# A ring of four decay buffers, PSUM evictions on VectorE, and one more identity product in each attention step of the first batch

## The reference

```python
x = x + gt_a * attention(modulated_norm(x))          # 16 heads of 16, causal
x = x + gt_m * (gelu(modulated_norm(x) @ W1 + b1) @ W2 + b2)
h, gate = adaln(x)                                   # second layer
x = x + gate * (ssm(h, fwd) + flip(ssm(flip(h), bwd)))
h, gate = adaln(x)
x = x + gate * ((silu(h @ w1) * (h @ w2)) @ w3)

def ssm(h):                                          # D_INNER 512, D_STATE 64
    xs, z = split(h @ in_w); xs = silu(xs)
    dt = softplus(xs @ xproj_w[:, :512] + dt_bias); Bm, Cm = the next 64 + 64 columns
    hst = hst * exp(dt * A) + (dt * xs) * B_t        # for each token and each of 64 states
    y_t = sum over states of hst * C_t
    return ((y + xs * D) * silu(z)) @ out_w
```

## Time and profile before

| | us |
|---|---|
| median of 3 runs | 3508.55 |
| lowest, highest | 3505.45, 3510.58 |
| the profiled execution | 3518.37 |
| its span, first to last instruction | 3516.6 |
| first scan starts | 213.1 |
| first batch's attention | 24.1 to 121.3 |

### The profile page before, as it was taken

One profiled execution on the slowest core, in us unless ns is written; L12 is line 12 of the kernel. 1 busy time (PEld: TensorE's weight loads), 2 busy tenths in 40 slices (PEclk: granted clock), 3 DMA queues, 4 the chain that ended last, 5 costly groups with the idle time before them and its releaser, 6 DMA issues.

```text
span 3516.6 us, 70442 instructions
## 1 busy us (share of the span) xinstructions
PE 3076.9 (87%) x21944; PEld 2674.0 (76%) x21944; DVE 2871.4 (82%) x3123; ACT 3087.7 (88%) x6821; POOL 2942.1 (84%) x1552
## 2 busy tenths in 40 slices
PE   8788898898988899898988989899898889988776
PEld 5567787787777788787877878778777778877765
DVE  2259988899888988789987998879988899789885
ACT  1279999999889999899998998999988999999995
POOL 0059988899888998889888998889988899899995
PEclk6689999999999999999999999999999999999999
DMA  4011111111111111111111111111111111111111
GB/s 168 0 37 45 46 41 47 40 52 43 41 47 47 45 44 41 46 47 46 42 40 49 48 45 40 48 39 52 44 40 48 47 45 43 42 42 44 53 48 27
DMA packets 163039, 162.55 MB, mean 46 GB/s; under 512 B 17610, under 2 KB 156874, under 8 KB 162644
## 3 DMA queue, kind: packets, MB, share of 16 engines
q1 hardware_dynamic: 162644, 157.69, 16.2%
HBM read 154.44 MB, written 3.18 MB: 45 GB/s over the span
## 4 chain that ended last, share of the span: by engine, by line
POOL 30%; PE 27%; issue 25%; ACT 12%; DVE 6%; POOLq 1%; DVEq 0%; ACTq 0%; DMA 0%; SPq 0%
POOL hst L409 23%; POOL uBT L418 7%; PE ps L1228 6%; PE ps L1244 6%; ACT dA L584 5%; PE ps L997 4%; ACT uBT L570 3%; DVE hst L899 3%; PE ps L1006 2%; PE ps L1066 2%; PE ps L1044 1%; PE ps L1117 1%; PE ps L1053 1%; PE ps L1127 1%; PE ps L1134 0%
## 5 line engine op out<-in xcount | busy, mean ns | idle before, releaser
L409 POOL TENSOR_TENSOR hst<-hst,C_sb 128x1024 f32<-128x1024 f32 x1024 | 2430.1, 2390 | 324.4 <-DVE hst L899 317.8
L899 DVE TENSOR_TENSOR_SCAN hst<-dA,ps 128x512 f32<-128x512 f32 x2048 | 2383.1, 1203 | 258.9 <-ACT dA L584 138.8
L584 ACT ACTIVATE dA<-dt,A 128x255 f32<-128x255 f32 x4096 | 1781.3, 501 | 105.9 <-DVE hst L899 100.4
L1228 PE MATMUL ps<-ident,uBT 128*128 128x128 f32 x8192 | 1276.2, 280 | 149.1 <-DVE hst L899 112.1
L1244 PE MATMUL ps<-ident,hst 128*128 128x128 f32 x8192 | 1274.9, 279 | 146.8 <-POOL hst L409 144.7
L1228 PEld LDWEIGHTS ps<-ident,uBT 128*128 128x128 f32 x8192 | 993.8, 145 | 283.0 <-DVE hst L899 146.2
L1244 PEld LDWEIGHTS ps<-ident,hst 128*128 128x128 f32 x8192 | 972.2, 144 | 209.3 <-POOL hst L409 207.9
L570 ACT ACTIVATE uBT<-uT,BT 128x512 f32<-128x512 f32 x1536 | 1046.7, 715 | 31.5 <-PE ps L1228 30.6
L418 POOL TENSOR_TENSOR uBT<-uT,BT 128x512 f32<-128x512 f32 x512 | 554.9, 1084 | 207.9 <-ACT uT L527 200.2
L485 ACT ACTIVATE probs<-ps,nmax 128x128 f32<-128x128 f32 (+1 forms) x256 | 105.4, 422 | 91.1 <-DVE nmax L770 91.1
L1066 PE MATMUL ps<-qk 32*128 32x256 f32 (+1 forms) x512 | 163.0, 400 | 0.6 <-DVE v L746 0.6
(11 more groups left out here) (143 smaller groups left out, 2150.7 us busy)
## 6 DMA issues: line engine op xcount, KB each, us to landing
C_sb<-c_dram SPq DMA_DIRECT2D x1024, 128.0 KB, 2.9
gate_l<-gate_rows_dram SPq DMA_DIRECT2D x16, 256.0 KB, 3.7
x_att<-in_x_dram SPq DMA_DIRECT2D x8, 256.0 KB, 3.2
w<-in_L_cond_W_dram SPq DMA_DIRECT2D x2, 1024.0 KB
out_dram<-x_glu SPq DMA_DIRECT2D x8, 256.0 KB, 3.1
wg<-in_L_cond_mlp_w_dram SPq DMA_DIRECT2D x3, 512.0 KB, 11.4
w_xp<-_L_cond_fwd_xproj_w_dram SPq DMA_DIRECT2D x1, 1280.0 KB, 12.5
w_xp<-_L_cond_bwd_xproj_w_dram SPq DMA_DIRECT2D x1, 1280.0 KB, 15.1
```

The source lines that it names most:

```text
L409: pool.tensor_tensor(h, h, C_sb[:, n % FED:n % FED + 1, :].to_broadcast([P, KI, NB]), ALU.mult).then_inc(hC_ready.sem, 1)
L584: done = act.activation(dA[:, n % NT, c, lo:hi], dt[:, d, c, lo:hi], ACT.Exp, scale=A[:, d, c, n:n + 1])
L899: dve.tensor_tensor_scan(pair(hst[:, n % NR]), pair(dA[:, n % NT]), ps[:, BANK_U + (2 * n + e) % (2 * NT), :][:, way], 0.0, ALU.mult, ALU. ...
L1228: last = pe.transpose(ps[:, BANK_U + (2 * n + e) % (2 * NT), o:o + P], uBT[:, n % NF, j, c * P:(c + 1) * P], ident[:, :])
```

## The change

Four things are changed.

1. In each step of `heads` for the first batch, PE multiplies the identity by the identity, fp32, 128x128, into a PSUM bank that is not used until the scans begin (BANK_WARM). That is 74 products.
2. The evictions of `norm` step 5, `dts` step 22 and `post` step 1 are done by DVE in place of ACT, at the same steps.
3. The ring `dA` has four states (NT = 4), and ACT makes the decays of state n + 2 (AHEAD = 2) while n is scanned. PE's banks for uB stay two states (NU = 2).
4. `o_sb`, `g_tok`, `mods` and `silu_col` have no memory of their own any more; they lie in `hT`, `gT` and `dt`.

```diff
-    NT = 2
-    NF, LEAD = 4, 3
+    NT, NU = 4, 2
+    NF, LEAD, AHEAD = 4, 3, 2
...
+    BANK_WARM = BANK_U + 3
...
+        o_sb = hT[:, :, :].rearrange("p k n -> p (k n)").rearrange("p (j d) -> p j d", d=D)
+        g_tok = gT[:, :, :].rearrange("p k n -> p (k n)").rearrange("p (j n) -> p j n", n=DI)
+        mods = dt[:, 1, 0, 0:8 * KD * B].rearrange("p (i k b) -> p i k b", k=KD, b=B)
+        silu_col = dt[:, 1, 1, 0:KD * B].rearrange("p (k b) -> p k b", b=B)
...
+        scan_done, hC_ready, y_mm = flow("scan_done", 2, 2 * NT), flow("hC_ready", 1, FED), flow("y_mm", 1, NR)
...
-                    if i == 5:
-                        act.wait_ge(xnT_mm[s].sem, xnT_mm[s].at(b, 1))
-                        for c in range(KD):
-                            col = bass.ds(b, 1)
-                            last = act.activation(dst[:, c, :], ps[:, BANK_P, c * NB:(c + 1) * NB], ACT.Identity,
-                                                  bias=mod_shift[:, s, c, col], scale=mod_scale[:, s, c, col])
-                        last.then_inc(hT_ready[s].sem, 1)
...
-                    if i == 22:
-                        act.wait_ge(uT_mm.sem, uT_mm.at(p, 1))
-                        act.activation(uT[:, d], ps[:, BANK_P:BANK_P + 2, :].rearrange("p a n -> p (a n)"), ACT.Copy).then_inc(uT_ready.sem, 1)
...
-                    if i == 1:
-                        act.wait_ge(gT_mm.sem, gT_mm.at(p, 1))
-                        act.activation(gT[:, :, :].rearrange("p k n -> p (k n)"), ps[:, BANK_P:BANK_P + 2, :].rearrange("p a n -> p (a n)"),
-                                       ACT.Copy).then_inc(gT_ready.sem, 1)
...
                 if r_known(p, n) >= NT:
-                    act.wait_ge(scan_done.sem, scan_done.at(p * NS + n, e + 1 - 2 * NT))
-                if n < NT:
-                    act.activation(dA[:, n, 2 * e:2 * e + 2, edge], zeros[:, :], ACT.Copy)
+                    act.wait_ge(scan_done.sem, scan_done.at(p * NS + n, (2 if n < NT else e + 1) - 2 * NT))
+                if n < NT and e == 0:
+                    act.activation(dA[:, n, :, edge], zeros[:, :], ACT.Copy)
                 for c in range(2 * e, 2 * e + 2):
...
-                    if n + 1 < NS:
-                        decays(p, d, n + 1, e)
+                    if n + AHEAD < NS:
+                        decays(p, d, n + AHEAD, e)
                     elif not last:
-                        decays(p + 1, 1 - d, 0, e)
+                        decays(p + 1, 1 - d, n + AHEAD - NS, e)
...
-            for e in range(2):
-                decays(0, 0, 0, e)
+            for n in range(AHEAD):
+                for e in range(2):
+                    decays(0, 0, n, e)
...
+                    if i == 5:
+                        dst = hT_ssm if s == LN_SSM else hT
+                        dve.wait_ge(xnT_mm[s].sem, xnT_mm[s].at(b, 1))
+                        dve.sem_inc(hT_turns)
+                        for c in range(KD):
+                            col = bass.ds(b, 1)
+                            last = dve.tensor_scalar(dst[:, c, :], ps[:, BANK_P, c * NB:(c + 1) * NB], mod_scale[:, s, c, col],
+                                                     mod_shift[:, s, c, col], ALU.mult, ALU.add)
+                        last.then_inc(hT_ready[s].sem, 1)
...
+                    if i == 22:
+                        dve.wait_ge(uT_mm.sem, uT_mm.at(p, 1))
+                        dve.tensor_copy(uT[:, d], ps[:, BANK_P:BANK_P + 2, :].rearrange("p a n -> p (a n)")).then_inc(uT_ready.sem, 1)
...
+                    if i == 1:
+                        dve.wait_ge(gT_mm.sem, gT_mm.at(2 * b + d, 1))
+                        dve.tensor_copy(gT[:, :, :].rearrange("p k n -> p (k n)"),
+                                        ps[:, BANK_P:BANK_P + 2, :].rearrange("p a n -> p (a n)")).then_inc(gT_ready.sem, 1)
...
+                    if isinstance(b, int) and b == 0:
+                        pe.matmul(ps[:, BANK_WARM, 0:P], ident[:, :], ident[:, :], start=True, stop=True)
...
-                if r_known(p, n) >= NT:
-                    pe.wait_ge(scan_done.sem, scan_done.at(r, e + 1 - 2 * NT))
+                if r_known(p, n) >= NU:
+                    pe.wait_ge(scan_done.sem, scan_done.at(r, e + 1 - 2 * NU))
```

More of the change, by code:

```diff
@@ L183, in cond_transformer_mamba_kernel @@
         ones_row, ones_bias = ones[0:1, :], ones[NS:NS + 1, :]
-        zeros = sb("zeros", [P, 2])
+        zeros = sb("zeros", [P, KI])
         skip_diag = sb("skip_diag", [P, 2, KI, P])
-        silu_col = sb("silu_col", [P, KD, B])
-        mods = sb("mods", [P, 8, KD, B])
         mod_scale = sb("mod_scale", [P, 4, KD, B])
@@ L207, in cond_transformer_mamba_kernel @@
         xn = probsT[:, :].rearrange("p (j d) -> p j d", d=D)
-        o_sb = sb("o_sb", [P, TT, D])
         prime = sb("prime", [P, 6])
@@ L214, in cond_transformer_mamba_kernel @@
         sz = sb("sz", [P, 2, TT, DI])
-        g_tok = sb("g_tok", [P, TT, DI])
         dt = sb("dt", [P, 2, KI, NB])
@@ L524, in prepare @@
                         act.activation(dt[:, d], channels(uT[:, d]), ACT.Ln).then_inc(log_ready.sem, 1)
-                    if i == 22:
-                        act.wait_ge(uT_mm.sem, uT_mm.at(p, 1))
-                        act.activation(uT[:, d], ps[:, BANK_P:BANK_P + 2, :].rearrange("p a n -> p (a n)"), ACT.Copy).then_inc(uT_ready.sem, 1)
                     yield
             def post(p):
-                for i in range(STEPS["post"]):
-                    if i == 1:
-                        act.wait_ge(gT_mm.sem, gT_mm.at(p, 1))
-                        act.activation(gT[:, :, :].rearrange("p k n -> p (k n)"), ps[:, BANK_P:BANK_P + 2, :].rearrange("p a n -> p (a n)"),
-                                       ACT.Copy).then_inc(gT_ready.sem, 1)
-                    yield
+                yield from idle(STEPS["post"])
             def glu(b):
@@ L546, in layer0 @@
             def layer0(b):
-                yield from norm(b, LN_ATT, hT)
+                yield from norm(b, LN_ATT)
                 yield from idle(STEPS["qkv"])
@@ L551, in layer0 @@
                 yield from idle(STEPS["proj"])
-                yield from norm(b, LN_MLP, hT)
+                yield from norm(b, LN_MLP)
                 yield from up(b)
                 yield from idle(STEPS["down"])
-                yield from norm(b, LN_SSM, hT_ssm)
+                yield from norm(b, LN_SSM)
             def close(b):
-                yield from norm(b, LN_GLU, hT)
+                yield from norm(b, LN_GLU)
                 yield from glu(b)
@@ L624, in period @@
                 scan_pass(b, 1, backwards, plan, not has_next)
-            for i, _ in enumerate(layer0(0)):
-                if i == 4:
-                    act.wait_ge(att_mods, 1)
-                if i == proj_at - 1:
-                    act.wait_ge(mods_ready, 1)
+            for _ in layer0(0):
+                pass
             act.wait_ge(ssm_in, N_SSM)
@@ L899, in state @@
                     dve.tensor_tensor_scan(pair(hst[:, n % NR]), pair(dA[:, n % NT]),
-                                           ps[:, BANK_U + (2 * n + e) % (2 * NT), :][:, way], 0.0, ALU.mult, ALU.add).then_inc(scan_done.sem, 1)
+                                           ps[:, BANK_U + (2 * n + e) % (2 * NU), :][:, way], 0.0, ALU.mult, ALU.add).then_inc(scan_done.sem, 1)
                 return state
@@ L1227, in force @@
                         o = c % 2 * NB + j * P
-                        last = pe.transpose(ps[:, BANK_U + (2 * n + e) % (2 * NT), o:o + P], uBT[:, n % NF, j, c * P:(c + 1) * P], ident[:, :])
+                        last = pe.transpose(ps[:, BANK_U + (2 * n + e) % (2 * NU), o:o + P], uBT[:, n % NF, j, c * P:(c + 1) * P], ident[:, :])
                 last.then_inc(uB_ready.sem, 1)
```

8 lines of the change are left out of this document (5 added, 3 removed).

## The result

The changed kernel takes 3529.0 us (median of four executions, 3527.9 to 3531.9) where the kernel before, timed beside it, takes 3508.9: a ratio of 1.0056, 95% interval 1.0037 to 1.0074. It is slower by 20 us; the forecast was 86 us faster, and the time lies outside the range. The profiled execution of after took 3527.9 us, its span is 3526.1. The profiled execution of before had been 9.8 us above its median, so the two spans differ by 9.5 us and not by 20.

A forecast was written before the change was run, and what follows sets the result against it. It took no single engine as the bound: four engines waiting for each other through a too short dA ring, plus a serial beginning at low clock. -153 +20 +20 for the passes, +27 for the beginning: -86, 3423 us; range 3335 to 3492.

The forecast's parts named there:

- (a) The products, +27: First batch's attention: 74 products cost 36.4 us of PE time, 8.2 covered by idle time; +27 us at the low clock.
- (b) The evictions, +40 on the path: Softplus and pass starts: 16 uT and 16 gT copies on DVE delay the scans, 20 us each; hT ones covered.
- (c) The ring, -153: Scan passes: ring of four gives back DVE's 138.8 us wait for dA and 14 us of its L521 wait.
- the second of the earlier trace: Beside attention's second half in a backward pass: PE busy 12.70 of 12.70 us, a stretch no ring can help.
- half of L521's wait: Scan passes: of DVE's 38.7 us wait for L521, 27.8 lie in the passes; half, 14 us, was credited.
- DVE the bound: Scan passes: everything waits for DVE, 144 us added and 96 returned, +48 and +27, 3584 us; chance 0.12.
- its turning point: In the passes: the DVE rival decides once DVE's waits for PE grow more than its waits for dA shrink.
- Clock held: First batch's attention: the products keep PE at 2.4 GHz, -25 us instead of +27, 3371 us; chance 0.23.
- Decoupling worth more: Scan passes: POOL's waits shrink by 195 us, 10 go to DVE's work, -185, 3351 us; chance 0.15.
- the pair of passes: Middle of the kernel: one forward and one backward pass together near 400 us instead of 416.
- wrong if DVE's waits for PE rise by more than 40 us: Scan passes: the forecast counts as wrong if DVE's waits for PE there rise by more than 40 us.
- the one on the passes beside attention: Passes beside attention: the forecast counts as wrong if these become shorter too.

The follow-up runs named there:

- e9: The changed kernel itself, unchanged, in a second set of eight executions: 3525.7 us, 1.0039 of the kernel before.
- e1: The kernel before with the 74 identity products alone; evictions, ring and memory as before: ratio 1.0074 to the kernel before.
- e2: The changed kernel without the 74 identity products: 3494.5 us, 0.9944 of the kernel before.
- e3: The changed kernel without the products and with the hT, uT and gT copies back on ACT: 0.9947 of the kernel before.
- e14: Ring of four and shared memory, ACT's interleaved steps ahead of its half-state's own work, copies on ACT, no products: 3478.8 us, 0.9901 of the kernel before.
- e11: The kernel before (ring of two) with only ACT's order changed, its interleaved steps ahead of its half-state's own work: 1.0059 of the kernel before.
- e8: The changed kernel with two identity products per step instead of one: 3491.7 us, 0.9940 of the kernel before.
- e12: The changed kernel with three identity products per step instead of one: 3489.1 us, 0.9932 of the kernel before.

## Why the prediction was wrong, point by point

- **(a) The products, +27.** Attention grew by 25 us in the profiled execution of after (13.7 in those of e9 and e1, where the clock rose once), and the group in the second half went from 5.69 to 7.11 us, against 1.95 - 0.21 = 1.74 us expected and 1.42 measured. The count and the cover were right, and the duration somewhat high (L1075, below, is busy 45.7 us for 74 products, with records that overlap their neighbours'). The 8.6 us by which the stretch behind attention became shorter came without products as well (e2) and belong to no term. What was missing is the passes: with the products they took 17.5 us more in e1 than in before and 20.5 more in after than in e2, with 25 and 55 us more at the low clock, and no term of the sum held that. In all the term is 24 to 39 us, by the medians and the ratios.
- **(b) The evictions, +40 on the path.** The durations were right: 16 uT copies in 19.1 us, 16 gT copies in 19.4 (39 expected), 64 of hT in 31.6 (31 expected).

```profile
L1075 PE MATMUL ps<-ident 128*128 128x128 f32 x148 | 45.7, 450 | 0.0
...
L714 DVE TENSOR_SCALAR hT<-ps,mod_scale,mod_shift 128x256 f32<-128x256 f32 x48 | 23.6, 533 | 16.6 <-PE ps L994 16.6
...
L842 DVE COPY gT<-ps 128x1024 f32<-128x1024 f32 x16 | 19.4, 1213 | 8.2 <-PE ps L1171 8.1
L835 DVE COPY uT<-ps 128x1024 f32<-128x1024 f32 x16 | 19.1, 1194 | 2.1 <-PE ps L1158 2.1
```

  The place was wrong. DVE was taken as last in line, but in the softplus ACT is the full engine (17.3 of 18.5 us before, 19.35 of 19.5 after), and what leaves ACT there is worth more than what DVE gains costs. Alone the evictions took 17.8 us off the passes. The wait for gT and uT did go, as said: 48.8 and 25.4 us became 8.2 and 2.1.
- **(c) The ring, -153.** This is the step that failed. The waits went as predicted (138.8 to 16.3, ACT's for scans 100.4 to 5.2 at L570), and the passes gained 15.6 us of it. The step took a wait between two engines for time on the path. In a line of four engines that are each 82 to 88% busy, most such waits stand beside a third engine that is full: of the 256 stretches of before ACT is the fullest in 96, PE in 88, POOL in 46 and DVE in 26. The text named one such stretch, the second of the earlier trace rows, and left it out of the sum. And half of L521's wait was booked as a gain; it grew by 20.5 us.
- **The sum.** -6 us for the passes where -113 stood, and +16 at the first scan where +27 stood. These 10 us are between the profiled executions; the medians differ by 20.
- **The rivals.** "DVE the bound" named the right direction for the wrong reason: its turning point was not reached, since DVE's waits for PE grew by 57 us and its waits for dA shrank by 122, and DVE is the fullest engine in 29 of the 256 stretches of after only. "Clock held" was in part seen: once for 23.9 us in e9 and e1, and wholly with three products, where it pays 10 to 21 us of attention against one product. The reason given for it, a full product in each step, fits, but it took more of them. "Decoupling worth more" is out: its 185 us are more than twice what lies over the fullest.
- **The signs.** Right: the clock of both halves near 0.5; waits for dA under 40; ACT's waits for scans gone; DVE's busy time 2929. Wrong: POOL's wait (310, not 200), the pair of passes (416, not 400), the first scan (229, not 240). And the line "wrong if DVE's waits for PE rise by more than 40 us" was met, and so was the one on the passes beside attention, as far as the backward passes go (2.6 us shorter in the middle pair).

The Trainium skill ("TensorE: Matmul & The Clock Gate", "Why this matters for your kernels") says to keep TensorE busy without gaps to have it at its full clock. These runs say that it isn't enough: PE was busy 62.90 of 62.90 us at a clock of 0.53 with one product a step, and the whole of attention was at 1.00 only with three.

## What to carry to other kernels

Before a wait is booked as a gain, cut the trace into stretches of a few tiles, take in each the length less the busy time of the fullest engine, and credit no more than the smaller of that and the wait's idle time in it: here 21 us, where the wait was 138.8 and the gain 15.6. Idle time belongs to the stretch in which it lies, which is the one before the scan that ends it. A deeper ring pays more together with an order that uses it, so that an engine does first what its partner waits for: 15.6 us of passes alone (e3), 33 with the order (e14), and the order without the ring cost 21 (e11). Filler products for the clock need a dose that holds it, or are better left out: here one a step cost 24 to 39 us, and three cost nothing (0.9932 against 0.9944 without any) but gained nothing clear of the intervals either. A single profile of each kernel doesn't show where 10 us went: here the same work gives a first scan at 203.9 or at 213.5 us.

## What the hardware showed that was not expected

- Full busy time at the low clock: PE worked without a gap for 62.9 us and the clock stayed at 0.53; 148 records in the heads did not lift it in after and lifted it for 23.9 us in e9, 444 kept it at 2.4 GHz for 112.6 us.
- The time at the low clock differs between executions of the same instructions: 214 to 279 us within the passes (e2, e8, e12, after, e9), which goes with 24 us of passes.
- Half of POOL's product (1292 ns instead of 2386 for a state) also made DVE's products between SBUF tiles cheaper (L832 from 2140 to 1218 ns): DVE's busy time fell from 2928.7 to 2872.8 us, with the 2048 scans at 1203 ns in both.
